# Latent attention with a gated feed-forward network on one core: maxima over adjacent score banks taken in one instruction, and small jobs and rope steps moved between units

## The chip, the cores and the metric

The kernel runs on one core of one Trainium2 chip. The metric is the device time of one execution in microseconds (us), lower being better.

## The reference

The input is x with 2048 tokens of 256 features. After a layer norm it goes through two branches whose product is added to x:

```python
xn = layernorm(x)
# attention, 16 heads, 128 plain + 64 rope features per query and key, latent width 64
q = xn @ wq; kva = xn @ wkv_a
ckv = rmsnorm(kva[:64]) * scale; k_pe = kva[64:]          # one rope key for all heads
k_nope, v = split(ckv @ wkv_b)
scores = causal([q_nope, rope(q_pe)] . [k_nope, rope(k_pe)] * 192**-0.5)
s = (softmax(scores) @ v) @ wo
# feed-forward, 704 hidden features
g = silu(down(silu(xn @ gate) * (xn @ up)))
out = x + s * g
```

## The kernel before, in words

Keys and values stay in latent form for all heads. `K_hi` and `K_lo` hold 64 rope and 64 latent key rows for the 2048 tokens, and each head's queries are brought into the same space (`wabs` is its key weight folded into the query weight, `wvo` its value weight folded into wo). Precision comes from splitting every operand into a high and a low part and multiplying three times.

**Units.** The attention is 8 pairs of heads, a pair is 16 units, so 128 units (`u`, and `k` from 0 to 15 within a pair: the key of all tables below). A unit is one head and one step (0 to 7), and a step takes two tiles of 128 queries: a late one, tile 15 - step, and an early one, tile step. The score columns of a unit are three spans: span 0, keys 0 to 1023 of the late tile; span 1, the remaining 1024 - 128 x step keys of the late tile; span 2, the 128 x (step + 1) keys of the early tile. Together they fill 2176 columns in five PSUM banks (`s_ps`): banks 0 and 1 hold span 0, the next one or two hold span 1, the others hold span 2. There is one copy of them, so unit u + 1 can write a bank only when the exponential of unit u has read it.

**What each engine does, in its own fixed order.** TensorE (PE), loop u: scores of u + 1 for spans 0 and 1, weighted values (`weigh`) of unit u - 2 for span 0, scores of u + 1 for span 2, `weigh` for spans 1 and 2, then the jobs of unit u. VectorE (DVE), loop u: the division by the row sums of a finished unit pair (`normalise`, every second unit), `row_max(u+1, 0)` and `row_max(u+1, 1)`, its part of the jobs of u - 1, the low half of one wide span (`prob_low`), `row_max(u+1, 2)`. ScalarE (ACT), loop u: exponentials of spans 0 and 1 (`exponentials`), high half of span 0 (`prob_high`), exponential of span 2, its part of the jobs of u - 1, in units 3, 5, 11 and 13 also `rope_high` (three copies of rotated query rows, which wait for POOL), high halves of spans 1 and 2. GpSimd (POOL), loop u: low halves of span 0 and of the smaller other span, then the steps that `steps_at(u)` lists. SyncE (SP), loop u: the four copies of `swap` if a `qB` job of u - 1 exists, then the two transposing DMAs of unit u's probabilities (`turn_first`, `turn_rest`), and the loads for the next pair.

**Maxima.** `exponentials` needs the negated row maximum `neg_max`. For the late tile `row_max` takes one maximum of span 0 (L941, as soon as its scores are there), one of span 1 (L941), and combines the two numbers (L944) after a wait on its own result; for the early tile one instruction does it (L939).

**Jobs** are the small matrix products and transposes beside the scores: query projections `qA3` to `qB0` (head A or B, query group 3, 0, 2, 1), weight preparation `wqT`, `wkvT`, `wabs`, `wvo`, outputs `outT` and `outP`. Each writes one of two PSUM slots (`slot_ps`) in turn, and PE waits in `slot` until the job before the last one has been read out by DVE or ACT. The dictionaries `JOBS_BEFORE`, `JOBS_OWN` and `JOBS_NEXT` give the unit of each job of the previous, the same or the next pair, at most two jobs to a unit.

**Rope** of query group g, both heads together: after the job `qBg` ACT has put the unrotated rows into `q_pe`, SP copies them with halves exchanged into `q_swap`, POOL does `rope g.0` (`pe` = q_pe x cos), `rope g.1` (q_swap x sin) and `rope g.2` (their sum), ACT makes the high parts (`rope_high`, fixed units), POOL the low parts (`A2lo`, `B2lo`). `POOL_OWN` and `POOL_NEXT` place the POOL steps:

```python
POOL_NEXT = {1: ["wkvs"], 6: ["wpe_hi"], 7: ["wpe_lo"], 10: rope(3), 11: ["A3lo", "B3lo"], 12: rope(0), 13: ["A0lo", "B0lo"]}
POOL_OWN = {2: rope(2), 3: ["A2lo", "B2lo"], 4: rope(1), 5: ["A1lo", "B1lo"]}
ROPE_HI_OWN, ROPE_HI_NEXT = {3: 2, 5: 1}, {11: 3, 13: 0}
```

Before the attention stand some 80 us of setup, behind it the feed-forward network, from about 985 us on.

Of the kernel before, what the change touches and what calls it, by code (L numbers as in the profile page):

```python
# [99 lines left out]
class Steps:  # L100
# [6 lines left out]
    def after(self, name):  # L107
# [69 lines left out]
def rope(g):  # L177
    return [f"rope{g}.{i}" for i in range(3)]
# [7 lines left out]
POOL_NEXT = {1: ["wkvs"], 6: ["wpe_hi"], 7: ["wpe_lo"], 10: rope(3), 11: ["A3lo", "B3lo"], 12: rope(0), 13: ["A0lo", "B0lo"]}  # L186
POOL_OWN = {2: rope(2), 3: ["A2lo", "B2lo"], 4: rope(1), 5: ["A1lo", "B1lo"]}
# [38 lines left out]
def mla_gated_ffn_kernel(nc, x, wq, wkv_a, wkv_b, wo, kv_scale, gate_w, up_w, down_w, gate_s, up_s,  # L226
                         down_s, cos_in, sin_in, cosT_in, sinT_in, out):
    with ExitStack() as ctx:
# [13 lines left out]
        def ab(name, shape, dt=F32):  # L242
            return sb(name, shape, dt, attn)
# [70 lines left out]
        part_max = ab("part_max", [P, 2, 2])  # L314
# [42 lines left out]
        scores_ready, part_done, max_ready = sem("scores_ready"), sem("part_done"), sem("max_ready")  # L357
# [519 lines left out]
        def _(dve):  # L877
# [392 lines left out]
```

## Time and profile before

| | us |
|---|---|
| median of three runs (lowest, highest) | 1112.69 (1109.94, 1112.72) |
| the profiled execution's own time | 1112.44 |
| its span, first to last instruction | 1110.6 |
| setup / eight pairs / feed-forward, read from the timelines | about 80 / 905 / 126 |
| one pair in the middle (313.08 to 426.64) | 113.56 |

A page's "busy" is the time in which an engine runs an instruction. An entry such as "[3.48 <-POOL pe L1102]" is idle time of the engine just before an instruction and what ended it. L numbers are lines of the kernel before. All element-wise operations of POOL carry L1102 and ACT's copies L725, so they are told apart by the names out<-in. "granted clock" or PEclk is TensorE's clock as a share of its full one.

### The profile page before, as it was taken

What the parts mean: (1) busy time and instruction counts of PE and PEld (TensorE: products, weight loads), DVE (VectorE), ACT (ScalarE), POOL (GpSimd) and SP (SyncE); (2) the same over time, 40 slices, a digit from 0 to 9 for tenths busy, and PEclk for the clock granted to TensorE, in tenths of its full rate; (3) what the DMA queues carried; (4) which work ended last, traced back from release to release, by engine and by line L of the source; (5) the groups of instructions that cost most, each with busy time, mean ns of one, the idle gap of its engine ahead of it and who ended that gap; (6) DMA issues with size and microseconds to landing.
All of it is one profiled execution on the core that took longest, in us unless ns stands there. A gap on an engine that the chain in (4) does not pass through costs nothing.

```text
span 1110.6 us, 26363 instructions
## 1 busy us (share of the span) xinstructions
PE 976.1 (88%) x10560; PEld 842.8 (76%) x10560; DVE 728.5 (66%) x1093; ACT 787.7 (71%) x1157; POOL 711.0 (64%) x514
## 2 busy tenths in 40 slices
PE   5738898989898989898989899998898898779998
PEld 5726786878787878786878787877787777768887
DVE  6546666767776767576767676777676776663134
ACT  1427878788887887787778878878888787763232
POOL 3455958486948694877487857776786667722331
PEclk8759998999999999999999989999899999889999
DMA  5018998989999999999989999999999989992001
GB/s 166 9 48 150 170 178 166 172 163 191 170 177 174 179 173 172 173 178 169 180 165 171 183 166 179 180 173 173 176 167 177 179 159 199 190 180 76 1 19 58
DMA packets 591978, 170.23 MB, mean 153 GB/s; under 512 B 574064, under 2 KB 585968, under 8 KB 591856
## 3 DMA queue, kind: packets, MB, share of 16 engines
q1 hardware_dynamic: 587376, 167.89, 83.7%
q8 instruction: 84, 1.38, 0.5%
q10 hardware_dynamic: 4480, 0.66, 0.4%
q14 instruction: 38, 0.31, 0.1%
HBM read 15.41 MB, written 2.10 MB: 16 GB/s over the span
## 4 chain that ended last, share of the span: by engine, by line
PE 27%; SPq 22%; POOL 16%; ACT 10%; issue 8%; DMA 8%; DVE 7%; ACTq 1%; POOLq 0%
SPq L465 10%; PE s_ps L620 10%; PE s_ps L522 9%; SPq L457 6%; DMA q_swap<-q_pe 5%; POOL hl L1102 5%; ACT hl L725 5%; SPq L451 4%; POOL pe L1102 4%; POOL q_swap L1102 4%; PE slot_ps L522 3%; ACT prob L802 2%; ACT QB_hi L725 2%; DVE part_max L941 2%; DVE hl L950 2%
## 5 line engine op out<-in xcount | busy, mean ns | idle before, releaser
L1102 POOL TENSOR_TENSOR hl<-prob,hl 128x1024 f16<-128x1024 f32 (+4 forms) x256 | 402.1, 1571 | 184.1 <-ACT hl L725 173.1
L802 ACT ACTIVATE prob<-s_ps,neg_max 128x1024 f32<-128x1024 f32 (+7 forms) x384 | 318.0, 862 | 95.1 <-DVE neg_max L944 74.4
L941 DVE TENSOR_REDUCE part_max<-s_ps 128x1 f32<-128x1024 f32 (+7 forms) x256 | 245.5, 988 | 176.6 <-PE s_ps L620 159.4
L725 ACT ACTIVATE hl<-prob 128x1024 f16<-128x1024 f32 (+7 forms) x384 | 296.3, 806 | 9.9 <-DMA pT<-hl 7.9
L636 PE MATMUL o_ps<-v,pT 128*128 128x65 f16 x2176 | 232.0, 195 | 7.1 <-DMA pT<-hl 5.7
L637 PE MATMUL o_ps<-v,pT 128*128 128x64 f16 x2176 | 232.5, 197 | 0.0
L638 PE MATMUL o_ps<-v,pT 128*128 128x65 f16 x2176 | 231.3, 193 | 0.0
L636 PEld LDWEIGHTS o_ps<-v,pT 128*128 128x128 f16 x2176 | 206.5, 98 | 7.8 <-DMA pT<-hl 6.3
L950 DVE TENSOR_TENSOR hl<-prob,hl 128x1024 f16<-128x1024 f32 (+3 forms) x128 | 158.3, 1236 | 78.0 <-ACT hl L725 76.5
L638 PEld LDWEIGHTS o_ps<-v,pT 128*128 128x128 f16 x2176 | 205.7, 100 | 0.0
L637 PEld LDWEIGHTS o_ps<-v,pT 128*128 128x128 f16 x2176 | 205.1, 98 | 0.0
L620 PE MATMUL s_ps<-K_hi,QB_hi 128*128 128x512 f32 (+3 forms) x320 | 133.4, 417 | 73.7 <-ACT prob L802 73.7
L620 PE MATMUL s_ps<-K_hi,QA_hi 128*128 128x512 f32 (+3 forms) x320 | 124.0, 387 | 16.4 <-DVE K_lo L887 9.7
L620 PEld LDWEIGHTS s_ps<-K_hi,QB_hi 128*128 128x128 f32 x320 | 65.9, 206 | 92.1 <-ACT prob L802 82.0
L620 PE MATMUL s_ps<-K_hi,QB_lo 128*128 128x512 f32 (+3 forms) x320 | 125.5, 392 | 0.0
L620 PE MATMUL s_ps<-K_lo,QB_hi 128*128 128x512 f32 (+3 forms) x320 | 124.9, 390 | 0.0
L620 PE MATMUL s_ps<-K_hi,QA_lo 128*128 128x512 f32 (+3 forms) x320 | 117.3, 367 | 0.0
L620 PE MATMUL s_ps<-K_lo,QA_hi 128*128 128x512 f32 (+3 forms) x320 | 117.2, 366 | 0.0
L939 DVE TENSOR_REDUCE neg_max<-s_ps 128x1 f32<-128x256 f32 (+7 forms) x128 | 96.4, 753 | 2.8 <-PE s_ps L623 0.9
L620 PEld LDWEIGHTS s_ps<-K_hi,QA_hi 128*128 128x128 f32 x320 | 61.0, 191 | 28.9 <-DVE K_lo L887 10.1
L725 ACT ACTIVATE QA_hi<-pe 64x512 fp32r<-64x512 f32 x32 | 20.2, 632 | 84.6 <-POOL pe L1102 84.6
L1234 POOL TENSOR_TENSOR hid_lo<-hid,hid_hi 128x512 fp32r<-128x512 f32 x24 | 31.4, 1307 | 74.1 <-ACT hid_hi L725 74.1
(182 smaller groups left out, 1974.8 us busy)
## 6 DMA issues: line engine op xcount, KB each, us to landing
q_swap<-q_pe SPq DMA_DIRECT2D x128, 64.0 KB, 2.1
pT<-hl SPq DMA_TRANSPOSE x256, 4.9
wq_sb<-in_L_attn_wq_dram SPq DMA_DIRECT2D x8, 384.0 KB, 4.1
acc<-in_L_attn_x_dram SPq DMA_DIRECT2D x4, 512.0 KB, 6.3
wo_sb<-in_L_attn_wo_dram SPq DMA_DIRECT2D x8, 256.0 KB, 4.0
x_in<-in_L_attn_x_dram SPq DMA_DIRECT2D x1, 2048.0 KB, 8.3
out_dram<-y SPq DMA_DIRECT2D x8, 256.0 KB, 2.1
wkvs<-in_L_attn_wkv_b_dram SPq DMA_DIRECT2D x8, 128.0 KB, 4.3
```

The lines of the kernel that those rows point to most:

```text
L465: sp.dma_start_transpose(pT12[:, u % 2], hl12[:, u % 2, :]).then_inc(turned12[u % 2], 16)
L522: last = nc.tensor.matmul(out_ap, a, b, start=(i == 0), stop=(i == n - 1))
L620: mm = nc.tensor.matmul(s_ps[:, b, 0:c], a[:, q], kk[:, k0 + c0:k0 + c0 + c], start=(j == 0), stop=(j == 2 and not ends))
L636: nc.tensor.matmul(whole, pT[:, b, :], v[:, kb, 0:LORA + 1], start=(m != 1 and b == 0), stop=False)
L637: nc.tensor.matmul(part, pT[:, b, :], v[:, kb, LORA + 1:VW], start=False, stop=False)
L638: last = nc.tensor.matmul(whole, pT[:, n + b, :], v[:, kb, 0:LORA + 1], start=False, stop=(m > 0 and b == n - 1))
L725: return nc.scalar.activation(dst, src, ACT.Copy)
L802: nc.scalar.activation(prob_of(u, m), score_bank(u, m), ACT.Exp, bias=neg_max[:, r:r + 1]).then_inc(exp_done, 1)
L939: nc.vector.tensor_reduce(neg_max[:, r:r + 1], src, AX.X, ALU.max, negate=True).then_inc(max_ready, 1)
L941: nc.vector.tensor_reduce(part_max[:, u % 2, m:m + 1], src, AX.X, ALU.max).then_inc(part_done, 1)
L950: nc.vector.tensor_tensor(both[:, w:2 * w], prob_of(u, m), both[:, 0:w], ALU.subtract).then_inc(lo_dve, 1)
L1102: return lambda: nc.gpsimd.tensor_tensor(dst, a, b, op)
```

## The change

Three things change. First, `row_max(u, 0)` now waits for the scores of spans 0 and 1, takes one maximum over the columns of both, which are contiguous across banks 0 to 2 or 3, and writes `neg_max` itself; the second maximum, the combination, the tile `part_max` and its semaphore are gone. Second, jobs move between units, most of them one or two units earlier: the query projections, `wkvT`, `wabs`; the output halves of `outP0` and `outP2` are put into two units, `outP1` and `outP3` come one unit earlier. `qA2` now belongs to unit 15 of the pair before, and in the first pair to unit 0 (`JOBS_FIRST`). Third, step 0 of each rope stands one unit earlier on POOL than steps 1 and 2, and for group 3 those stay in unit 10 while its projections come one unit earlier; `wpe_lo` joins `wpe_hi` in unit 6. `rope_high` keeps its units.

```diff
-JOBS_BEFORE = {2: ["outT3"], 4: ["outP3a", "outP3b"]}
-JOBS_OWN = {0: ["qA2"], 1: ["qB2"], 2: ["qA1"], 3: ["qB1"], 5: ["wvo"], 6: ["outT0"], 7: ["outP0a", "outP0b"], 10: ["outT1"],
-            12: ["outP1a", "outP1b"], 14: ["outT2"], 15: ["outP2a", "outP2b"]}
-JOBS_NEXT = {3: ["wqT"], 5: ["wkvT"], 6: ["wabs"], 8: ["qA3"], 9: ["qB3"], 10: ["qA0"], 11: ["qB0"]}
-FFN_COUNT = {8: 1, 9: 2, 10: 1, 11: 2, 13: 2, 14: 1, 15: 2}
+JOBS_BEFORE = {0: ["outP2b"], 2: ["outT3"], 3: ["outP3a", "outP3b"]}
+JOBS_OWN = {0: ["qB2"], 1: ["qA1"], 2: ["qB1"], 5: ["wvo"], 6: ["outT0"], 7: ["outP0a"], 8: ["outP0b"], 10: ["outT1"],
+            11: ["outP1a", "outP1b"], 14: ["outT2"], 15: ["outP2a"]}
+JOBS_NEXT = {4: ["wqT", "wkvT"], 5: ["wabs"], 7: ["qA3"], 8: ["qB3"], 9: ["qA0"], 10: ["qB0"], 15: ["qA2"]}
+JOBS_FIRST = {0: ["qA2"]}
+FFN_COUNT = {8: 1, 9: 2, 10: 1, 12: 2, 13: 2, 14: 1, 15: 2}
...
-POOL_NEXT = {1: ["wkvs"], 6: ["wpe_hi"], 7: ["wpe_lo"], 10: rope(3), 11: ["A3lo", "B3lo"], 12: rope(0), 13: ["A0lo", "B0lo"]}
-POOL_OWN = {2: rope(2), 3: ["A2lo", "B2lo"], 4: rope(1), 5: ["A1lo", "B1lo"]}
+POOL_NEXT = {1: ["wkvs"], 6: ["wpe_hi", "wpe_lo"], 9: rope(3)[:1], 10: rope(3)[1:], 11: ["A3lo", "B3lo"] + rope(0)[:1], 12: rope(0)[1:],
+             13: ["A0lo", "B0lo"]}
+POOL_OWN = {1: rope(2)[:1], 2: rope(2)[1:], 3: ["A2lo", "B2lo"] + rope(1)[:1], 4: rope(1)[1:], 5: ["A1lo", "B1lo"]}
...
             def row_max(u, m):
-                src = score_bank(u, m)
+
                 r = (2 * u + m // 2) % 4
-                dve.wait_ge(scores_ready, scores_through(u, m))
-                if m == 2:
-                    nc.vector.tensor_reduce(neg_max[:, r:r + 1], src, AX.X, ALU.max, negate=True).then_inc(max_ready, 1)
-                    return
-                nc.vector.tensor_reduce(part_max[:, u % 2, m:m + 1], src, AX.X, ALU.max).then_inc(part_done, 1)
-                if m == 1:
-                    dve.wait_ge(part_done, 2 * u + 2)
-                    nc.vector.tensor_reduce(neg_max[:, r:r + 1], part_max[:, u % 2, :], AX.X, ALU.max, negate=True).then_inc(max_ready, 1)
+                src = score_bank(u, 2) if m else s_ps[:, 0:2 + len(banks(u, 1)), :].rearrange("p b c -> p (b c)")[:, 0:W0 + width(u, 1)]
+                dve.wait_ge(scores_ready, scores_through(u, m or 1))
+                nc.vector.tensor_reduce(neg_max[:, r:r + 1], src, AX.X, ALU.max, negate=True).then_inc(max_ready, 1)
...
                 if u + 1 < NU:
                     row_max(u + 1, 0)
-                    row_max(u + 1, 1)
```

The order on the engines moves at three places that matter. The first is DVE at the turn from one pair to the next (L913 reads out an output half `outP`, L897 a query projection; the L950 of before is L945 now). Before:

```order
L941 TENSOR_REDUCE part_max<-s_ps 128x1 x2
L944 TENSOR_REDUCE neg_max<-part_max 128x1
L913 TENSOR_TENSOR acc<-slot_ps,acc 128x2x256 x2
L950 TENSOR_TENSOR hl<-prob,hl 128x1024
L939 TENSOR_REDUCE neg_max<-s_ps 128x1
```

Now, from the same maximum on:

```order
L939 TENSOR_REDUCE neg_max<-s_ps 128x1
L913 TENSOR_TENSOR acc<-slot_ps,acc 128x2x256
L897 TENSOR_TENSOR QA_lo<-slot_ps,QA_hi 64x512
L945 TENSOR_TENSOR hl<-prob,hl 128x1024
L939 TENSOR_REDUCE neg_max<-s_ps 128x1 x2
L913 TENSOR_TENSOR acc<-slot_ps,acc 128x2x256
L897 TENSOR_TENSOR QB_lo<-slot_ps,QB_hi 64x512
```

Two neighbouring units now hold two jobs each, where one held two and the next one. The three maxima of the late tile have become one.

The second is POOL in units 1 and 2 (hl are low halves, pe and q_swap rope steps, POOL's L1102 is L1096 now). Before:

```order
L1102 TENSOR_TENSOR wkvs<-wkvs,scale_sb 64x512
L1102 TENSOR_TENSOR hl<-prob,hl 128x1024
L1102 TENSOR_TENSOR hl<-prob,hl 128x256
L1102 TENSOR_TENSOR pe<-q_pe,cosT 128x512
L1102 TENSOR_TENSOR q_swap<-q_swap,sinT 128x512
L1102 TENSOR_TENSOR pe<-pe,q_swap 128x512
```

Now:

```order
L1096 TENSOR_TENSOR pe<-q_pe,cosT 128x512
L1096 TENSOR_TENSOR wkvs<-wkvs,scale_sb 64x512
L1096 TENSOR_TENSOR hl<-prob,hl 128x1024
L1096 TENSOR_TENSOR hl<-prob,hl 128x256
L1096 TENSOR_TENSOR q_swap<-q_swap,sinT 128x512
L1096 TENSOR_TENSOR pe<-pe,q_swap 128x512
```

The product with the cosines went ahead of unit 1's `wkvs`; two rope steps are left behind unit 2's low halves instead of three.

The third is PE at the end of units 3 and 4 of the first pair (L536 is `wqT`, L540 `wkvT`, the L522 rows here the projection `qB`, which moved to the unit before):

```order
 L637 MATMUL o_ps<-v,pT 128x64
 L638 MATMUL o_ps<-v,pT 128x65
+L536 MATMUL slot_ps<-ident,wq_sb 128x128 x4
+L540 MATMUL slot_ps<-ident,wkvs 128x128 x4
 L620 MATMUL s_ps<-K_hi,QA_hi 128x512
 L620 MATMUL s_ps<-K_lo,QA_hi 128x512
```

Both weight transposes now follow each other in unit 4, where each needs a slot that unit 3's jobs have left.

## Rows read from the trace of the kernel before

**Rows 1.** The page: busy time of each engine over the whole span
```profile
PE 976.1 (88%) x10560; PEld 842.8 (76%) x10560; DVE 728.5 (66%) x1093; ACT 787.7 (71%) x1157; POOL 711.0 (64%) x514
```

**Rows 2.** One pair, 313.08:426.64: engines' busy us, granted clock, DMA share, GB/s
```profile
313.08:426.64 113.56, 103.47 (x1221) 88.77 (x1220) 82.41 (x118) 92.48 (x135) 81.30 (x56) 0.97 0.99 174
```

**Rows 3.** Waits inside that pair: who for whom, us in total, times, longest
```profile
PE s_ps L620 <- ACT prob L802: 9.8, 5, 3.4
...
ACT QA_hi L725 <- POOL pe L1102: 8.6, 4, 3.5
```

**Rows 4.** Timelines of POOL, ACT and DVE around the stall of units 3 and 4
```profile
334.09 1.28 POOL L1102 TENSOR_TENSOR q_swap<-q_swap,sinT 128x512 f32<-128x512 f32 x1 [1.73 <-DMA q_swap<-q_pe]
335.46 1.29 POOL L1102 TENSOR_TENSOR pe<-pe,q_swap 128x512 f32<-128x512 f32 x1
...
336.78 0.63 ACT L725 ACTIVATE QA_hi<-pe 64x512 fp32r<-64x512 f32 x1 [3.48 <-POOL pe L1102]
...
332.41 2.09 DVE L941 TENSOR_REDUCE part_max<-s_ps 128x1 f32<-128x1024 f32 x2 [1.49 <-PE s_ps L620]
...
343.46 1.22 DVE L941 TENSOR_REDUCE part_max<-s_ps 128x1 f32<-128x1024 f32 x1 [1.66 <-PE s_ps L620]
```

**Rows 5.** Windows of 2 us: PE in that stall and just after it
```profile
338.00:340.00 2.00, 0.00 (x0) 0.00 (x0) 0.43 (x1) 1.95 (x5) 0.96 (x2) 1.00 0.89 199
...
342.00:344.00 2.00, 2.00 (x6) 1.60 (x5) 0.54 (x1) 1.96 (x4) 1.84 (x3) 0.50 1.08 177
```

**Rows 6.** Timelines of ACT and DVE around the stall of unit 11
```profile
392.39 0.63 ACT L725 ACTIVATE QA_hi<-pe 64x512 fp32r<-64x512 f32 x1 [1.90 <-POOL pe L1102]
...
389.40 1.56 DVE L941 TENSOR_REDUCE part_max<-s_ps 128x1 f32<-128x1024 f32 x2 [1.41 <-PE s_ps L620]
...
399.62 1.56 DVE L941 TENSOR_REDUCE part_max<-s_ps 128x1 f32<-128x1024 f32 x2 [1.35 <-PE s_ps L620]
```

**Rows 7.** Timeline of DVE, unit 1, up to unit 2's first maximum
```profile
313.08 1.23 DVE L941 TENSOR_REDUCE part_max<-s_ps 128x1 f32<-128x1024 f32 x1 [1.36 <-PE s_ps L620]
314.51 1.22 DVE L941 TENSOR_REDUCE part_max<-s_ps 128x1 f32<-128x1024 f32 x1 [0.21 <-PE s_ps L623]
315.77 0.16 DVE L944 TENSOR_REDUCE neg_max<-part_max 128x1 f32<-128x2 f32 x1
...
319.65 1.23 DVE L941 TENSOR_REDUCE part_max<-s_ps 128x1 f32<-128x1024 f32 x1 [1.19 <-PE s_ps L620]
```

**Rows 8.** DVE instructions by form: the widest and the narrowest maximum
```profile
L941 DVE TENSOR_REDUCE part_max<-s_ps 128x1 f32<-128x1024 f32 x144 | 176.4, 1225 | 171.1 <-PE s_ps L620 159.4 <-PE s_ps L623 11.2
...
L941 DVE TENSOR_REDUCE part_max<-s_ps 128x1 f32<-128x128 f32 x16 | 4.5, 280 | 0.0
```

**Rows 9.** Timelines of DVE and PE where a pair's unit 0 has just ended
```profile
421.41 1.22 DVE L941 TENSOR_REDUCE part_max<-s_ps 128x1 f32<-128x1024 f32 x1 [1.70 <-PE s_ps L623]
...
422.74 0.68 DVE L887 TENSOR_TENSOR oT_lo<-slot_ps,oT_hi 128x512 fp32r<-128x512 f32 x1
...
423.57 0.36 PE L522 MATMUL slot_ps<-wvo_hi,oT_hi 128*128 128x256 f32 x1 [0.19 <-DVE oT_lo L887]
```

**Rows 10.** The chain that ended last, at the turn of a pair
```profile
418.48 1.12 ACT prob L802
...
419.64 1.66 PE s_ps L620 x6
```

**Rows 11.** SP queue lines in one pair: count, ns min/median/max
```profile
L457 SPq DMA_TRANSPOSE pT<-hl x16: 1317/2276/3651, 315.3 to 422.2; - x16
...
L465 SPq DMA_TRANSPOSE pT<-hl x17: 2687/3242/4285, 311.0 to 425.3; - x17
...
L451 SPq DMA_DIRECT2D q_swap<-q_pe x16: 542/583/591, 330.1 to 402.5; - x16
```

**Rows 12.** Timeline of DVE: one low half of 1024 columns, slow and fast
```profile
414.95 2.36 DVE L950 TENSOR_TENSOR hl<-prob,hl 128x1024 f16<-128x1024 f32 x1 [0.23 <-ACT hl L725]
...
423.34 1.22 DVE L950 TENSOR_TENSOR hl<-prob,hl 128x1024 f16<-128x1024 f32 x1
```

More of the change, by code:

```diff
@@ L140, in jobs_at @@
         last = pair == PAIRS - 1
-        if pair > 0:
-            jobs += [(name, pair - 1) for name in JOBS_BEFORE.get(k, ())]
+        jobs += [(name, pair - 1) for name in JOBS_BEFORE.get(k, ())] if pair > 0 else [(name, pair) for name in JOBS_FIRST.get(k, ())]
         jobs += [(name, pair) for name in JOBS_OWN.get(k, ()) if (name, pair) not in OUT_LAST]
@@ L313, in mla_gated_ffn_kernel @@
         identb = ab("identb", [P, P], BF16)
-        part_max = ab("part_max", [P, 2, 2])
         neg_max = ab("neg_max", [P, 4])
@@ L356, in mla_gated_ffn_kernel @@
         swapped, rope_hi = sem("swapped"), sem("rope_hi")
-        scores_ready, part_done, max_ready = sem("scores_ready"), sem("part_done"), sem("max_ready")
+        scores_ready, max_ready = sem("scores_ready"), sem("max_ready")
         exp_done, prob_hi = sem("exp_done"), sem("prob_hi")
```

## The prediction

> **What bounds the kernel now.** I read the page's busy shares first, then one whole pair, then the waits in it, then the timelines where they fall. TensorE (PE) is busy 88% of the span, ACT 71%, DVE 66% [rows 1]. A middle pair takes 113.56 us with PE busy 103.47 at a mean granted clock of 0.97 [rows 2]. A pair is what repeats: seven full turns of it, and a last pair without projections for a next one.
>
> What PE would need at full clock is 103.47 less what the clock cost, 0.03 x 113.56 = 3.4, so 100.1 us. The other 13.5 of a pair are 10.1 of idle time and 3.4 of clock. The waits say where the idle time sits: five waits of PE for an exponential, 9.8 us, and four waits of ACT for POOL's last rope step, 8.6 us [rows 3]. They are one thing. In unit 3 ACT reached `rope_high` and sat 3.48 us until POOL's `pe` was done; SP's copies had been late for POOL by 1.73 before that [rows 4]. ACT works in order, so the exponentials of unit 4 came late, PE stood still (0.00 busy at 338 to 340), and just afterwards its granted clock was 0.50, the lower of its two levels, 1.2 GHz [rows 5]. DVE's first maximum, which starts when span 0 is ready, stands 11.05 us after the one before (332.41 to 343.46) [rows 4]; the calm distance in the same pair is 6.57 (313.08 to 319.65) [rows 7]. Unit 11 repeats it: ACT waits 1.90, and the maxima stand 10.22 apart (389.40 to 399.62) [rows 6].
>
> **Part 1, the rope.** Steps 1 and 2 stay behind the low halves, but step 0, 1.3 us like its neighbours [rows 4], runs a unit earlier, where POOL has idle time, and the copies that feed step 1 are issued a unit earlier. In unit 3 `pe` then ends 1.3 us (the step) plus 1.73 (the wait for the copies) earlier, 3.0 of the 3.48 waited. In unit 11, whose projections too come a unit earlier, the 1.90 goes whole. I take all of the 13.5 us as removed and add back what stays or comes. The bounds of the removal: nothing, if ACT would be late by its own work, and 13.5. I take the upper end because the waits for `pe` in ACT's queue are the rows directly ahead of both large stalls.
>
> What stays for ACT: `rope_high` is three copies of 0.63 [rows 4], 1.9 us. ACT's 92.48 over 16 units [rows 2] less these is 5.3 a unit, 7.2 with them, against PE's 100.1 / 16 = 6.3: 0.9 of backlog in each of four units. After an exponential of span 0 PE has 0.9 to spare (worked out under part 3), which covers three of them. The fourth, unit 13, now follows units 12 and 13 without any job, and jobs are some 1.35 of PE's 6.3, so backlog meets a unit of 4.9: 1.4 us. With 0.3 for unit 5, which gets two weight copies: **1.7 us a pair**.
>
> **Part 2, the maximum by itself.** A maximum of 1024 columns takes 1225 ns, one of 128 takes 280 [rows 8]: 1.055 ns a column and 0.15 us fixed. No row has more than 1024 columns or crosses from span 0 into span 1; extended, 2048 columns take 2.31 us, with 2.31 to 2.45 (two whole ones) as the ends, and I take 2.31 because every form lies on that line. Per unit DVE saves 0.15 fixed and 0.16 for the combination. But it starts later. In unit 1 span 0 was ready at 313.08, span 1 at 314.51, and `neg_max` stood at 315.93, 1.42 after span 1 [rows 7]. Now it stands 2.31 after it: **0.9 later at 2048 columns**, shrinking to about 0.1 at 1152, since then span 1 is ready soon after span 0.
>
> **Part 3, where that is paid.** The first candidate is the exponential. It takes 1.12 for spans of 1024, and six score matmuls of span 0 take 1.66 [rows 10]. So in unit 1 it ends at 315.93 + 1.12 = 317.05, and PE starts the next span 0 at 319.65 - 1.66 = 317.99 [rows 7]: 0.94 of spare against 0.9 more. Just covered; if the cover is gone, each unit pays the difference (the third rival). The second is the slot. A job must wait until DVE has read out the job two before it, which stands behind the maximum in DVE's queue. At the turn of a pair PE got there already 0.19 too early: span 1 ready at 421.41, DVE's job after the maxima at 422.74, PE's matmul at 423.57 [rows 9]. PE alone needs 423.38 - 421.41 = 1.97 from span 1 to its jobs; DVE's path took 2.16, of which 0.94 is not the maximum, 0.79 without the combination. Now it is 2.31 + 0.79 = 3.10, so PE waits 1.13. And the table now puts two jobs into each of units 15, 0, 2, 3, 4 with one in unit 1, so that there is a slot wait in each; before, the units between held one job. Unit by unit (the maximum shrinks by 0.135 a step; PE's way, an estimate, grows by 0.15 because span 2 grows): unit 15, 1.13 - 0.19 = 0.94; unit 0, 1.13; unit 1, 0.85; unit 2, 0.3 (only its second job waits); unit 3, 0.5; unit 4, 0.65, `wqT` and `wkvT` both waiting. From step 3 on the two ways are equal. **Sum 4.4 us a pair.** Ends: 0, if DVE keeps ahead, and 6 x 1.13 = 6.8.
>
> **Part 4, the rest.** A low half on DVE took 1.22 or 2.36 [rows 12], the long one while POOL worked. DVE's later start gives new meetings of that kind; between 0 and 4 a pair, each 1.14; I take about one, **1.0**. The Trainium skill, SBUF — State Buffer, section "Who interferes with whom", says a VectorE instruction with two SBUF inputs contends with a GpSimd one that reads SBUF, that a tensor_reduce never does, and that issue order decides who blocks. By that rule the merged maximum itself stays at its length, and four such meetings in place of one would bring 7 x 3.4 = 24 us on the sum below. SP: medians of 2.28 and 3.24 for the transposes of a unit and 0.58 for a copy [rows 11] make 16 x 5.52 + 16 x 0.58 = 97.6 us a pair; no instruction is added, but the swap moves past one unit's transposes and stands ahead of `turn_first` of units 1, 3, 9, 11. In units 12 and 13, 4.9 long, the queue falls behind by 2 x 0.6, partly buffered by the two copies of the turned tiles: **0.8**. The other moved jobs keep their lengths on every engine and lie inside the 100.1.
>
> **The sum.** A pair: 100.1 + 4.4 + 1.7 + 1.0 + 0.8 = 108.0, against 113.56, so 5.56 less. Seven times that is 39. In the last pair two rope stalls go and the same slot waits come: nothing. 1112.44, the profiled execution's own time, less 39 gives **1073 us**; the median, 1112.69, is the same within 0.3.
>
> **The rivals.** (A) As forecast, 1055 to 1090, chance 0.63.
>
> (B) No slot waits: if span 1's maximum were short enough for PE, a pair takes 103.6 and the time is 1112 - 7 x 10 = 1043. For it speaks that PE waited for a slot only 0.19 before; against, that DVE's queue there leaves no slack at all. The Trainium skill, Perfetto Trace Analysis, section "Identifying the Most-Contended Engine", would have one look at the most occupied engine, and DVE is the third here; by that rule its longer path costs nothing. 0.12.
>
> (C) Slower: ACT's own load, not its wait, makes the stalls. Place: the units after 3, 5, 11 and 13. `exponentials` now starts up to 0.9 later, the spare of 0.94 is used up, so ACT's backlog falls on PE in full and all 13.5 us stay, with the 4.4 of slot waits on top, less the 0.19: 1112 + 7 x 4.2 = 1142. It decides from the point where the rope's move frees less than 4.4 us a pair. ACT is at 81% of the pair, which speaks for it; the wait of 3.48 in one piece speaks against. 0.10.
>
> (D) The change does only half of what it says: SP's queue, with its maxima of 3.65 and 4.29 [rows 11], needs up to 107 us a pair once PE runs on, and it idles for some 4 in units 0 and 1. Then a pair takes 111 and the time is 1095. 0.15.
>
> **How the numbers follow.** Range 1045 to 1103: A and D whole with the second meeting of part 4, and the upper edge of B; left out are C and most of B. A measurement can tell about 0.3%, 3.3 us. Slower is C, 0.10, and 0.02 for mishaps of the new order; 0.04 falls within 0.3%, between D and C; faster 0.84.
>
> **What would show it.** Right: ACT's waits for `pe` under 2 us a pair; no window at a granted clock of 0.50 behind unit 3 or 11; the group of maxima at 2.3 us for 2048 columns; PE waits on `slot_ps` for DVE of 4 us a pair in units 15 to 4; distances of 7 to 8 us between the late tile's maxima there. Wrong: idle PE before `s_ps` still near 10 us a pair (C), `slot_ps` waits near 0 (B), or SP without gaps (D).

## The result: slower by 1.25%, and the profile after

| | before | after |
|---|---|---|
| median, us (lowest, highest) | 1111.44 (1109.94, 1112.72) | 1125.77 (1120.64, 1128.94) |
| ratio to before, 95% interval | | 1.0125 [1.0078, 1.0172] |
| span of the profiled execution, us | 1110.6 | 1127.0 |
| mean granted clock | 0.943 | 0.955 |

The forecast was 1073 us, faster. The changed kernel is slower, outside the range and on the other side. The page of after, busy time and the chain that ended last:

```profile
PE 978.6 (87%) x10560; PEld 840.2 (75%) x10560; DVE 699.3 (62%) x837; ACT 789.3 (70%) x1157; POOL 714.7 (63%) x514
...
PE 36%; DVE 15%; POOL 15%; ACT 13%; issue 8%; DMA 8%; SPq 5%; ACTq 1%; POOLq 0%
```

Against [rows 1] DVE has 256 instructions and 29 us of work less, the others are as they were, and the time is longer. One operation marks the pairs well: the division of a finished unit pair, eight to a pair of heads. The first and the 57th of them, and the last, in DVE's timeline of after:

```profile
116.40 0.17 DVE L954 RECIPROCAL rinv<-o_ps 128x4 f32<-128x4 f32 x1
...
925.20 0.17 DVE L954 RECIPROCAL rinv<-o_ps 128x4 f32<-128x4 f32 x1
...
1016.14 0.18 DVE L954 RECIPROCAL rinv<-o_ps 128x4 f32<-128x4 f32 x1 [7.09 <-PE o_ps L638]
```

and of before:

```profile
112.17 0.17 DVE L959 RECIPROCAL rinv<-o_ps 128x4 f32<-128x4 f32 x1
...
909.54 0.17 DVE L959 RECIPROCAL rinv<-o_ps 128x4 f32<-128x4 f32 x1
...
1000.72 0.18 DVE L959 RECIPROCAL rinv<-o_ps 128x4 f32<-128x4 f32 x1 [8.27 <-PE o_ps L638]
```

The seven turns between the first two take 808.8 us, 115.54 each, against 797.4, 113.91 each. So 11.4 of the 16.4 us of span lie in the turns, 4.2 ahead of them (1.3 of these ahead of the first exponential, 82.92 against 81.64), and 0.7 behind them. This mean of seven turns is called the length of a pair from here on. TensorE over the seven turns, after and before, in the windows view:

```profile
116.40:925.20 808.80, 723.75 (x8545) 618.87 (x8546) 542.88 (x602) 650.24 (x940) 573.58 (x386) 0.99 0.97 172
```

```profile
112.17:909.54 797.37, 725.12 (x8525) 623.47 (x8526) 569.86 (x826) 647.72 (x939) 568.87 (x385) 0.96 0.99 174
```

PE is busy 103.4 us a pair after and 103.6 before; its idle time is 12.15 against 10.32. So the added time is idle time of PE. One middle pair of after in the windows view, for [rows 2]:

```profile
313.46:427.81 114.35, 101.80 (x1220) 87.12 (x1220) 77.89 (x87) 92.84 (x135) 82.41 (x55) 1.00 0.97 174
```

PE is idle for 12.55 us of it, where it was 10.1. The waits in it, for [rows 3]:

```profile
DVE neg_max L939 <- PE s_ps L623: 27.3, 15, 3.4
ACT prob L802 <- DVE neg_max L939: 19.9, 16, 2.5
...
PE s_ps L620 <- ACT prob L802: 8.2, 6, 2.7
ACT QA_hi L725 <- POOL pe L1096: 2.8, 2, 1.6
...
PE slot_ps L522 <- DVE acc L913: 1.8, 2, 1.0
PE slot_ps L522 <- DVE oT_lo L887: 1.6, 2, 1.1
...
PE slot_ps L522 <- DVE QA_lo L897: 0.4, 1, 0.4
...
PE slot_ps L536 <- DVE acc L913: 0.5, 1, 0.5
```

These are the whole account. PE's waits for a slot are 1.8 + 1.6 + 0.5 + 0.4 = 4.3 us, its waits for an exponential 8.2, and 4.3 + 8.2 = 12.5. The slot waits are new and of the size forecast. The waits for an exponential were 9.8 before and should have fallen to about 3.5. DVE's instructions by form, widest and narrowest merged maximum, for [rows 8]:

```profile
L939 DVE TENSOR_REDUCE neg_max<-s_ps 128x1 f32<-128x2048 f32 x16 | 36.7, 2292 | 56.4 <-PE s_ps L623 56.4
...
L939 DVE TENSOR_REDUCE neg_max<-s_ps 128x1 f32<-128x1152 f32 x16 | 21.6, 1350 | 6.2 <-PE s_ps L623 6.2
```

**Where the old stalls went.** ACT's timeline in unit 3 of that pair, for [rows 4]:

```profile
336.67 2.02 ACT L802 ACTIVATE prob<-s_ps,neg_max 128x1024 f32<-128x1024 f32 x2 [1.26 <-DVE neg_max L939]
338.57 1.05 ACT L725 ACTIVATE hl<-prob 128x1024 f16<-128x1024 f32 x1
339.52 0.47 ACT L802 ACTIVATE prob<-s_ps,neg_max 128x256 f32<-128x256 f32 x1
339.87 0.60 ACT L725 ACTIVATE oT_hi<-slot_ps 128x512 fp32r<-128x512 f32 x1
340.50 0.59 ACT L725 ACTIVATE q_pe<-slot_ps 64x512 f32<-64x512 f32 x1
341.11 0.59 ACT L725 ACTIVATE QB_hi<-slot_ps 64x512 fp32r<-64x512 f32 x1
341.72 0.63 ACT L725 ACTIVATE QA_hi<-pe 64x512 fp32r<-64x512 f32 x1
...
343.54 1.26 ACT L725 ACTIVATE hl<-prob 128x896 f16<-128x896 f32 x2
344.82 1.12 ACT L802 ACTIVATE prob<-s_ps,neg_max 128x1024 f32<-128x1024 f32 x1
```

The wait of 3.48 for `pe` is gone, as forecast. But ACT is busy without a gap from one exponential to the next, 344.82 - 336.67 = 8.15 us: this unit carries `rope_high` and three more copies of 0.6 for two jobs. Unit 11 has the same picture, 8.36 us (391.57 to 399.93). It was so before as well: there ACT's exponentials of units 3 and 4 stood at

```profile
328.42 2.02 ACT L802 ACTIVATE prob<-s_ps,neg_max 128x1024 f32<-128x1024 f32 x2 [0.36 <-DVE neg_max L944]
...
339.87 1.91 ACT L802 ACTIVATE prob<-s_ps,neg_max 128x1024 f32<-128x1024 f32 x2
```

and 11.45 less the wait of 3.48 [rows 4] leaves 7.97 us of ACT's own work. In unit 5 the wait is still there. ACT and POOL:

```profile
356.99 0.63 ACT L725 ACTIVATE QA_hi<-pe 64x512 fp32r<-64x512 f32 x1 [1.56 <-POOL pe L1096]
```

```profile
345.69 2.02 POOL L1096 TENSOR_TENSOR QA_lo<-pe,QA_hi 64x512 fp32r<-64x512 f32 x1
347.79 1.28 POOL L1096 TENSOR_TENSOR QB_lo<-pe_b,QB_hi 64x512 fp32r<-64x512 f32 x1
349.15 1.28 POOL L1096 TENSOR_TENSOR pe<-q_pe,cosT 128x512 f32<-128x512 f32 x1
350.51 3.72 POOL L1096 TENSOR_TENSOR hl<-prob,hl 128x1024 f16<-128x1024 f32 x2
354.31 1.28 POOL L1096 TENSOR_TENSOR q_swap<-q_swap,sinT 128x512 f32<-128x512 f32 x1
355.67 1.28 POOL L1096 TENSOR_TENSOR pe<-pe,q_swap 128x512 f32<-128x512 f32 x1
```

POOL has no gap for 11 us here, so step 0 in an earlier unit is still in front of step 2, and the swapped rows, which no longer come late, change nothing. The exponentials stand 9.13 apart (350.83 to 359.96); in unit 13, with the same picture, 9.61 (404.74 to 414.35).

### The profile page after: what moved, and what is told of

The parts are those of the page before. It is cut to its first block, busy times and chain, and to the rows that moved or that the text cites. A ratio compares the mean times of both kernels' runs of the same rounds, so it can differ in the third digit from the quotient of the medians.

```text
span 1127.0 us, 26107 instructions
## 1 busy us (share of the span) xinstructions
PE 978.6 (87%) x10560; PEld 840.2 (75%) x10560; DVE 699.3 (62%) x837; ACT 789.3 (70%) x1157; POOL 714.7 (63%) x514
## 4 chain that ended last, share of the span: by engine, by line
PE 36%; DVE 15%; POOL 15%; ACT 13%; issue 8%; DMA 8%; SPq 5%; ACTq 1%; POOLq 0%
PE s_ps L620 15%; PE s_ps L522 9%; DVE neg_max L939 9%; POOL hl L1096 6%; PE slot_ps L522 6%; ACT hl L725 5%; DMA pT<-hl 5%; ACT prob L802 4%; DVE hl L945 3%; POOL pe L1096 3%; POOL q_swap L1096 2%; ACT QB_hi L725 2%; SPq L465 2%; PE o_ps L522 2%; POOL QA_lo L1096 1%
## 5 line engine op out<-in xcount | busy, mean ns | idle before, releaser
L1096 POOL TENSOR_TENSOR hl<-prob,hl 128x1024 f16<-128x1024 f32 (+4 forms) x256 | 399.5, 1561 | 250.3 <-ACT hl L725 240.5
L939 DVE TENSOR_REDUCE neg_max<-s_ps 128x1 f32<-128x1792 f32 (+15 forms) x256 | 329.0, 1288 | 245.1 <-PE s_ps L623 243.2
L725 ACT ACTIVATE hl<-prob 128x1024 f16<-128x1024 f32 (+7 forms) x384 | 296.5, 807 | 12.7 <-DMA pT<-hl 10.6
L636 PE MATMUL o_ps<-v,pT 128*128 128x65 f16 x2176 | 229.1, 193 | 5.4 <-DMA pT<-hl 3.3
L637 PE MATMUL o_ps<-v,pT 128*128 128x64 f16 x2176 | 229.7, 196 | 0.0
L638 PE MATMUL o_ps<-v,pT 128*128 128x65 f16 x2176 | 228.6, 192 | 0.0
L945 DVE TENSOR_TENSOR hl<-prob,hl 128x1024 f16<-128x1024 f32 (+3 forms) x128 | 161.8, 1264 | 62.0 <-ACT hl L725 59.8
L620 PE MATMUL s_ps<-K_hi,QB_hi 128*128 128x512 f32 (+3 forms) x320 | 129.5, 405 | 46.6 <-ACT prob L802 46.6
L620 PE MATMUL s_ps<-K_hi,QB_lo 128*128 128x512 f32 (+3 forms) x320 | 121.9, 381 | 0.0
L620 PEld LDWEIGHTS s_ps<-K_hi,QB_lo 128*128 128x128 f32 x320 | 64.1, 200 | 10.7
L620 PEld LDWEIGHTS s_ps<-K_lo,QB_hi 128*128 128x128 f32 x320 | 64.1, 200 | 10.5
```

What stands on the lines that cost most here:

```text
L620: mm = nc.tensor.matmul(s_ps[:, b, 0:c], a[:, q], kk[:, k0 + c0:k0 + c0 + c], start=(j == 0), stop=(j == 2 and not ends))
L636: nc.tensor.matmul(whole, pT[:, b, :], v[:, kb, 0:LORA + 1], start=(m != 1 and b == 0), stop=False)
L637: nc.tensor.matmul(part, pT[:, b, :], v[:, kb, LORA + 1:VW], start=False, stop=False)
L638: last = nc.tensor.matmul(whole, pT[:, n + b, :], v[:, kb, 0:LORA + 1], start=False, stop=(m > 0 and b == n - 1))
L725: return nc.scalar.activation(dst, src, ACT.Copy)
L945: nc.vector.tensor_tensor(both[:, w:2 * w], prob_of(u, m), both[:, 0:w], ALU.subtract).then_inc(lo_dve, 1)
```

## The experiments

Ratios are to the kernel before on the same chip in the same minutes. Waits are PE's over the whole run, from the waits view: "exp" for an exponential, "slot" for a slot in the attention. Pair and waits come from one profiled execution each, which can lie some us off the median (6 to 7 below it for e1, g1 and g4, 4 above it for e2). The value of a ratio in us is taken on 1112.

| run | median us | ratio [95%] | pair us | exp | slot |
|---|---|---|---|---|---|
| before | | | 113.91 | 80.4 | 1.4 |
| after | 1125.77 | 1.0125 [1.0078, 1.0172] | 115.54 | 65.9 | 32.1 |
| e1_merge_only | 1121.71 | 1.0100 [1.0069, 1.0130] | 114.61 | 65.7 | 25.6 |
| e2_table_only | 1095.93 | 0.9852 [0.9820, 0.9885] | 112.14 | 67.9 | 3.0 |
| e3_jobs_only | 1109.70 | 0.9985 [0.9971, 1.0000] | 113.94 | 72.8 | 8.5 |
| e4_late_start | 1129.13 | 1.0156 [1.0132, 1.0179] | 116.02 | 59.3 | 37.0 |
| e5_max_first | 1096.33 | 0.9864 [0.9843, 0.9884] | 112.66 | 65.5 | 5.8 |
| e6_two_back | 1097.42 | 0.9877 [0.9859, 0.9894] | 112.17 | 69.4 | 3.0 |
| e7_pool_relief | 1071.72 | 0.9644 [0.9626, 0.9662] | 108.97 | 53.7 | 3.0 |
| e8_after_max_first | 1119.18 | 1.0072 [1.0053, 1.0091] | 115.14 | 55.0 | 32.1 |
| f1_after_relief | 1103.50 | 0.9935 [0.9913, 0.9958] | 112.67 | 49.3 | 32.1 |
| f2_after_jobs_first | 1127.71 | 1.0151 [1.0125, 1.0177] | 115.59 | 94.1 | 0.6 |
| f3_cos_on_dve | 1078.22 | 0.9683 [0.9644, 0.9723] | 109.29 | 54.9 | 3.0 |
| f4_cos_merged_jobs_first | 1117.31 | 1.0059 [1.0037, 1.0081] | 114.33 | 86.2 | 0.6 |
| g1_table_late | 1142.43 | 1.0270 [1.0232, 1.0307] | 117.79 | 63.3 | 43.7 |
| g5_table_merge_narrow | 1093.23 | 0.9817 [0.9790, 0.9845] | 111.65 | 66.1 | 3.0 |
| g6_table_merge_wide | 1124.32 | 1.0113 [1.0073, 1.0154] | 115.83 | 69.8 | 32.1 |
| g4_cos_merge_narrow | 1078.03 | 0.9676 [0.9631, 0.9720] | 109.08 | 55.6 | 3.0 |

### The two halves apart

**e1_merge_only** is the kernel before with the new `row_max` and nothing else.

> The kernel before with the merged maximum alone, its own tables. Theory T1 (the maximum costs: neg_max 0.9 us later at 2048 columns falls on PE through slots and through the exponential): slower, 1118 to 1135 us, the calm distance between late-tile exponentials in units 0 to 3 grows by 0.3 to 0.9 us each, and PE waits on slot_ps for DVE grow from 0.2 to 1 to 3 us a pair. Theory T2 (the maximum is nearly free in the old table, the new table is what costs): within 5 us of before, 1107 to 1116.

**e2_table_only** is the changed kernel with the two maxima and their combination put back: all tables new.

> The kernel after with the two separate maxima and their combination back, all new tables kept. T1: the slot waits of about 4 us a pair go, the rope gain stays, so faster than before: 1080 to 1095 us. T2: the table itself is no better than the old one: 1110 to 1125 us, with the exponentials of units 5 to 6 and 13 to 14 still 9 us apart as they are in the kernel after.

**e3_jobs_only** is e2 with the POOL tables of before:

```diff
+POOL_NEXT = {1: ["wkvs"], 6: ["wpe_hi"], 7: ["wpe_lo"], 10: rope(3), 11: ["A3lo", "B3lo"], 12: rope(0), 13: ["A0lo", "B0lo"]}
+POOL_OWN = {2: rope(2), 3: ["A2lo", "B2lo"], 4: rope(1), 5: ["A1lo", "B1lo"]}
```

> As the table-only kernel, but POOL keeps the order of before: the jobs moved, the rope steps not. T1 (moving rope step 0 ahead is what frees ACT): ACT's wait for POOL's pe in unit 3 comes back with 1 to 3 us and the time is 5 to 20 us above the table-only kernel. T2 (the moved steps stand ahead of the next unit's low half on a POOL that has no room, which costs as much as they bring): equal to the table-only kernel within 5 us, or faster.

The merged maximum costs 11 us on the old tables and 1.0125 - 0.9852, 30 us, on the new ones. The tables bring 16 us. The jobs' moves alone bring 2 (the interval of e3 reaches 1.0000), the POOL moves on top the rest. A part of that rest may only repair what e3 itself opens: its query projections come a unit earlier while `wpe_lo` stays in unit 7, and PE waits 5.5 us over the run for POOL's `wc_lo`, a wait that neither before nor e2 has. The forecast had 70 us for the tables (7 x 13.5, less 3.5 a pair of residues) and -31 for the slots. In e2 a middle pair still has these rows, windows view and waits:

```profile
313.00:425.60 112.60, 103.35 (x1221) 89.24 (x1220) 83.21 (x118) 93.07 (x134) 81.31 (x56) 0.97 1.00 176
```

```profile
PE s_ps L621 <- ACT prob L803: 9.0, 5, 2.7
PE slot_ps L523 <- DVE oT_lo L888: 0.2, 1, 0.2
```

Of the 9.8 us of [rows 3] 9.0 are left, and the clock stays at 0.97. That is the failure of the forecast in one line. PE's timeline says where they sit. Before, the waits behind units 3 and 5:

```profile
341.04 0.50 PE L620 MATMUL s_ps<-K_hi,QB_hi 128*128 128x512 f32 x1 [3.43 <-ACT prob L802]
...
356.08 0.50 PE L620 MATMUL s_ps<-K_hi,QB_hi 128*128 128x512 f32 x1 [0.74 <-ACT prob L802]
```

and in e2, behind units 3 and 5 and in and behind unit 13:

```profile
332.17 0.50 PE L621 MATMUL s_ps<-K_hi,QB_hi 128*128 128x512 f32 x1 [1.11 <-ACT prob L803]
347.11 0.50 PE L621 MATMUL s_ps<-K_hi,QB_hi 128*128 128x512 f32 x1 [2.39 <-ACT prob L803]
...
397.60 0.50 PE L621 MATMUL s_ps<-K_hi,QA_hi 128*128 128x512 f32 x1 [1.52 <-ACT prob L803]
402.90 0.79 PE L621 MATMUL s_ps<-K_hi,QB_hi 128*128 128x512 f32 x1 [2.74 <-ACT prob L803]
```

The two large stalls did shrink, in unit 3 from 3.43 to 1.11 and in unit 11 from 2.45 to 1.21, 3.6 us together. Those of units 5 and 13 grew, from 0.74 to 2.39 and from 1.98 to 1.52 + 2.74 = 4.26, 3.9 us together. (A wait of 1.19 at the end of the pair went.) So the stall moved more than it went.

### What the rest of the stalls is made of

**e6_two_back** is e2 with step 0 of the ropes of groups 1 and 0 back beside the other steps:

```diff
-... 9: rope(3)[:1], 10: rope(3)[1:], 11: ["A3lo", "B3lo"] + rope(0)[:1], 12: rope(0)[1:],
+... 9: rope(3)[:1], 10: rope(3)[1:], 11: ["A3lo", "B3lo"], 12: rope(0),
...
-... 3: ["A2lo", "B2lo"] + rope(1)[:1], 4: rope(1)[1:],
+... 3: ["A2lo", "B2lo"], 4: rope(1),
```

> Table-only kernel with rope step 0 of groups 1 and 0 put back behind the next unit's low halves (units 4 and 12), while those of groups 2 and 3 stay early. T4 (POOL works without a gap from unit 3 to 5 and 11 to 13, so the place of a step within that stretch does not change when its last step ends): within 4 us of the table-only kernel. If moving step 0 ahead did help there, as my forecast took for granted: 5 to 12 us slower.

It makes no difference (0.9877 against 0.9852, intervals overlap, pair 112.17 against 112.14). Where POOL has no gap, a step's place in it is worth nothing.

**e7_pool_relief** is e2 with POOL's sine product cut from 512 columns to one.

```diff
-... tt(q_swap[:, n % 2, :], q_swap[:, n % 2, :], sinT[:, query_cols(g)], ALU.mult)
+... tt(q_swap[:, n % 2, 0:1], q_swap[:, n % 2, 0:1], sinT[:, g * BANK:g * BANK + 1], ALU.mult)
```

> Table-only kernel with rope step 1 cut to one column: the product with the sines is left out for the other 511 columns, POOL is relieved of 1.2 us four times a pair. T4: ACT's waits for pe, 31 us, fall below 10 and the time to 1070 to 1085 us. T3: the waits for pe fall too, but the low halves still meet POOL: 1085 to 1094 us.

Four times 1.3 us less on POOL shorten a pair by 3.2 us and the run by 23. (The other 511 columns are left out, so this kernel computes something else; it only measures what the time on POOL is worth.) Of the 3.2 us 1.3 are idle time of PE; 1.9 are PE's busy time, 101.4 against 103.3 us a pair, with the granted clock over the seven turns at 0.99 against 0.97. Its middle pair:

```profile
297.40:405.82 108.42, 100.86 (x1222) 86.99 (x1221) 83.55 (x118) 93.09 (x136) 77.56 (x55) 1.00 1.03 183
```

The exponentials of unit 5 now stand 8.72 apart (9.79 in e2), those of unit 13 8.67 (9.77), those of unit 3 8.59 (8.74). PE's waits of units 5 and 13 fell from 2.39 to 0.71 and from 4.26 to 3.16. So in units 5 and 13 POOL holds a share of the stall; in unit 3 the distance stays near the 8.15 that ACT's own instructions fill in the timeline above. PE waits 53.7 us for exponentials even here.

**f3_cos_on_dve** relieves POOL as well, with nothing left out: DVE makes the cosine product right behind the low half of `qB`.

```diff
-    return [f"rope{g}.{i}" for i in range(3)]
+    return [f"rope{g}.{i}" for i in (1, 2)]
...
+                    nc.vector.tensor_tensor(pe[:, n % 2, :], q_pe[:, n % 2, :], cosT[:, query_cols(g)], ALU.mult).then_inc(rope_cos, 1)
```

> Table-only kernel in which rope step 0, the product with the cosines, is done by DVE right behind the job qB (0.7 us there, 1.3 on POOL), four times a pair; nothing is left out. If POOL's load makes the remaining stalls, 1072 to 1085 us, close to the pool-relief kernel. If what helps there was only the shorter way from SP's copies to pe: 1090 to 1098 us.

It is 3.2% faster than before and 4.4% faster than the changed kernel. The product, by form, in this kernel and in the one before:

```profile
L909 DVE TENSOR_TENSOR pe<-q_pe,cosT 128x512 f32<-128x512 f32 x32 | 22.7, 709 | 1.0
```

```profile
L1102 POOL TENSOR_TENSOR pe<-q_pe,cosT 128x512 f32<-128x512 f32 x32 | 47.3, 1478 | 9.5 <-issue 7.0
```

**e5_max_first** and **e8_after_max_first** tested another suspect, DVE's early-tile maximum behind its low half, which meets POOL and is then slow (2.29 at 405.82 in after, where POOL was already at work; 1.09 at 414.48, where it began 0.01 ahead of POOL's `QA_lo`, and that took 2.23 in place of 1.28). The two change places in e2 and in the changed kernel:

```diff
-                if 0 <= u < NU:
-                    prob_low(u, 3 - smaller(u))
                 if u + 1 < NU:
                     row_max(u + 1, 2)
+                if 0 <= u < NU:
+                    prob_low(u, 3 - smaller(u))
```

> Table-only kernel (two maxima, new tables) with one swap on DVE: the early tile's maximum of unit u+1 goes ahead of the low half of unit u. Theory T3 (what is left of the stalls comes through DVE: a low half of 2.2 to 2.5 us that meets POOL holds up the early tile's maximum, so ACT's exponential of span 2 and all behind it come late in units 5, 13 and 15): 1075 to 1088 us, ACT's waits for the early tile's neg_max, 37 us, fall below 15, and the exponentials after unit 5 and unit 13 stand under 9 us apart instead of 9.8. Rival T4 (ACT and POOL have no room in these units, whatever DVE does): 1092 to 1100 us.

> The kernel after (merged maximum, new tables) with the same swap on DVE as the first kernel here. If the slot waits set the loss of the merged maximum, it stays 25 to 32 us above the first kernel: 1103 to 1118 us; if the loss ran through the early tile's maximum, the two come within 12 us of each other.

On e2 nothing came of it: ACT's wait for that maximum fell from 36.8 to 7.5 us over the run, its waits for `pe` and for the turning DMAs rose from 31 and 18 to 42 and 32. On the changed kernel it brought 6 us, and the intervals overlap.

### Why the merged maximum costs 30 us

**f1_after_relief** is the changed kernel with e7's edit.

> The kernel after (merged maximum, new tables) with rope step 1 cut to one column as in the pool-relief kernel: the sine product is left out for the other 511 columns. If the two losses are independent (slot waits of about 4.4 us a pair, and POOL's load), the merged maximum costs 25 to 32 us here too: 1097 to 1104 us. If the slot waits only count because POOL is full, or if POOL's stalls hide them: under 1090 us.

0.9935 against e7's 0.9644: the merged maximum costs 32 us with POOL relieved, as it does without. So the two losses are separate and add up.

**f2_after_jobs_first** is the changed kernel, where DVE does its part of the jobs of u - 1 ahead of the merged maximum, so that a slot is free early:

```diff
-                if u + 1 < NU:
-                    row_max(u + 1, 0)
                 if u <= NU:
                     for name in jobs_at(u - 1):
                         job(name)
+                if u + 1 < NU:
+                    row_max(u + 1, 0)
```

> The kernel after, in which DVE reads out the jobs of unit u-1 ahead of the merged maximum of unit u+1, in time in which it only waited for the scores. If PE's waits for a slot are the price of the merged maximum, they fall from about 4 us a pair to under 1 and the time comes to 1095 to 1106 us. If the price runs through the later exponential, it stays at 1118 to 1128 us. A third way: the jobs wait for ACT's copies where ACT is late (units 3, 5, 11), and the maximum now waits behind them: 1105 to 1118.

The slot waits are gone (0.6) and the time is the same. PE now waits 94.1 us for exponentials, 72 times instead of 47. DVE's timeline ahead of unit 1's exponential in the third pair shows the new path:

```profile
318.35 0.69 DVE L897 TENSOR_TENSOR QA_lo<-slot_ps,QA_hi 64x512 fp32r<-64x512 f32 x1 [1.98 <-ACT QA_hi L725]
319.07 2.29 DVE L939 TENSOR_REDUCE neg_max<-s_ps 128x1 f32<-128x2048 f32 x1
```

DVE stands 1.98 for ACT's copy, and the maximum then starts behind it. In this unit the last product of span 1 ended at 318.29 + 0.23 = 318.52, so the maximum starts 0.5 late and `neg_max` stands 2.84 us after span 1, where the changed kernel has 2.29. So f2 frees the slots and makes `neg_max` later at once. It shows that a free slot does not help if the maximum pays for it; no run frees the slots and leaves the maximum where it is.

**f4_cos_merged_jobs_first** joins the three edits: merged maximum, jobs first, cosine product on DVE.

> The kernel after with both repairs: cosine product on DVE, jobs read out ahead of the merged maximum. If both theories hold: within 8 us of the kernel with the cosines on DVE and two maxima, 1072 to 1090 us. If the merged maximum still costs something of its own, 1090 to 1110.

42 us slower than f3, again with the waits at the exponential.

**e4_late_start** and **g1_table_late** test the lateness alone. Both keep the two maxima; the first one also waits for span 1. e4 is on the kernel before, g1 on e2.

```diff
-                dve.wait_ge(scores_ready, scores_through(u, m))
+                dve.wait_ge(scores_ready, scores_through(u, max(m, 1)))
```

> The kernel before, in which the first maximum also waits for span 1: the lateness of the merged maximum without its saving. neg_max comes 1.2 us later than before at 2048 columns, 0.3 later than merged. T1: slower than the merge-only kernel by 2 to 10 us, and most of the merge-only loss is the late start. T2: like the merge-only kernel within 4 us.

> The new tables with two maxima; the only edit is that the maximum of span 0 also waits for the products of span 1, so it starts as late as the merged maximum does, with nothing of DVE's other work or of the slots' jobs changed in order. T5 (the 30 us that the merged maximum costs on the new tables are its lateness: neg_max is ready later, and DVE, whose work between two units cannot run ahead any more, passes that on): 1123 to 1135 us, at least as slow as the changed kernel (1125.8), since the extra instruction is kept. T6 (the price is the single long reduction that holds the slots' jobs back, and lateness alone costs little): 1098 to 1110, near the tables alone (1095.9).

g1 is 46 us slower than e2 by one wait, with the same instructions in the same order. PE pays it in the slots: those waits rise by 40.7 us over the run, the waits for exponentials fall by 4.6. DVE's timeline, unit 1:

```profile
315.57 2.35 DVE L942 TENSOR_REDUCE part_max<-s_ps 128x1 f32<-128x1024 f32 x2 [3.42 <-PE s_ps L624]
317.96 0.15 DVE L945 TENSOR_REDUCE neg_max<-part_max 128x1 f32<-128x2 f32 x1
```

The same place in the changed kernel, with the two job instructions behind it:

```profile
319.32 2.29 DVE L939 TENSOR_REDUCE neg_max<-s_ps 128x1 f32<-128x2048 f32 x1 [3.42 <-PE s_ps L623]
321.53 0.68 DVE L913 TENSOR_TENSOR acc<-slot_ps,acc 128x512 f32<-128x512 f32 x1
322.24 0.69 DVE L897 TENSOR_TENSOR QA_lo<-slot_ps,QA_hi 64x512 fp32r<-64x512 f32 x1
```

`neg_max` stands 1.42 us after span 1 in the kernel before [rows 7], 2.29 in the changed one and 317.96 + 0.15 - 315.57 = 2.54 in g1; in e2 it is 1.41, as before. Pairs of 112.14 (e2), 115.54 and 117.79 us go with these. It is lateness that costs. Joining the instructions gives a part back, by ratio 6 us on the old tables (e4 to e1) and 16 on the new ones (g1 to the changed kernel); it spares an instruction and 0.25 us of the lateness, and the runs do not part the two.

**g5_table_merge_narrow** and **g6_table_merge_wide** put the merged maximum into one half of a pair's units.

```diff
+                merged = step_of(u) >= HALF // 2
+                if merged and m == 0:
+                    return
+                if merged and m == 1:
+                    src = s_ps[:, 0:2 + len(banks(u, 1)), :].rearrange("p b c -> p (b c)")[:, 0:W0 + width(u, 1)]
```

> The new tables, with the merged maximum only in the steps 4 to 7 of a pair (units 8 to 15), where it reads 1536 to 1152 columns; units 0 to 7 keep two maxima. T5a (every unit pays for the lateness, since DVE and ACT alternate in all of them): about half of the 30 us, 1108 to 1113. T5b (the price sits in the first half, where the slots' jobs wait behind a reduction of 1.8 to 2.3 us): 1093 to 1101, no dearer than the tables alone (1095.9), or gained by the instruction left out.

> The mirror image: the merged maximum only in the steps 0 to 3 of a pair (units 0 to 7, 2048 to 1664 columns), two maxima in the rest. T5a: 1108 to 1113 as well. T5b: 1120 to 1127, the whole price. Its difference and that of the mirror image from the tables alone should add up to the 30 us if the halves do not help each other.

(g6 has `<`.) The narrow half costs nothing (0.9817 against 0.9852: 4 us better by the ratios, the intervals overlap), the wide half costs 29 us. The sum, 25, is 5 short of the 30, which the intervals allow.

**g4_cos_merge_narrow** is f3 with g5's edit.

> The fastest version so far (new tables, two maxima, the cosine product on DVE; 1078.2 us) with the merged maximum in steps 4 to 7 only. T5b: 1070 to 1079, since DVE is spared one instruction a unit where nothing waits behind the maximum. T5a: 1088 to 1096.

It equals f3. The best version found is f3, or g4, at 1078 us.

## Why the prediction was wrong, step by step

**What bounds the kernel.** "They are one thing" was half right. PE's stalls did follow ACT's waits for `pe`, but those waits stood in front of two further limits, ACT's own work in units 3 and 11 (7.97 us in unit 3 before, where PE's share of a pair is 6.3) and POOL's gapless stretches ahead of units 5 and 13.

**Part 1, the failed step:** "I take all of the 13.5 us of a pair as removed". The tables alone took 113.91 - 112.14 = 1.8 us off a pair. The shares of the step: the 3.0 of 3.48 in unit 3 did go, and ACT's waits for `pe` fell from 8.6 [rows 3] to 2.8 us, above the 2 that was named as the mark. The time did not follow: the waits behind units 3 and 11 fell by 3.6 us in e2 and those of units 5 and 13 rose by 3.9. The residue for ACT, 1.7 us, was worked out from a mean of 7.2 us for a unit with `rope_high`; the unit that matters took 8.15, because three copies of two jobs fall into it, as they did before. POOL's residue was put at nothing, with no more reason than that step 0 runs "where POOL has idle time"; e7 and f3 show it worth some 3 us a pair. Residues of 1.7 + 1.0 + 0.8 = 3.5 stand against 8.2 us of measured waits for exponentials. Against the forecast pair of 108.0, the measured 115.54 is 7.5 longer: 4.2 of that is idle time of PE (12.15 where 4.4 + 3.5 was forecast), and 3.3 is the other term of the step, the clock. The sum took all 3.4 us of clock as given back and PE at 100.1. PE was busy 103.4 a pair although the granted clock over the seven turns rose from 0.96 to 0.99, and 101.8 in the pair at 1.00.

**Part 2** held: 2.31 forecast for 2048 columns, 2.29 measured, and 1.35 at 1152. `neg_max` came 0.9 later.

**Part 3** held in size: slot waits of 4.4 a pair forecast, 4.3 in the pair and 32.1 over eight of them measured. The cover of 0.94 at the exponential also held in the changed kernel: in units 0 to 4 of the middle pair PE waits for no exponential. But in f2, with the slots freed and the maximum behind the jobs, PE pays the same at the exponential. The merged maximum cost 30 us in all, forecast 31, while on the old tables it costs 11, since PE's waits for exponentials fell there by 14.7 as the slot waits rose by 24; on the new tables they fell by 2.0 against 29.1. That these were stalls which would have come anyway a little later is my reading, not shown.

**Part 4.** A low half took 2.29 (unit 13) and 2.36 (unit 15) where POOL was at work first, and 1.09 and 1.23 otherwise, and the maxima kept their lengths: 2.02 for 1792 columns at 341.58, POOL idle for 3.02 behind its low half, and again 2.02 at 348.77 with POOL at work. By the rule of the Trainium skill, SBUF — State Buffer, section "Who interferes with whom", both should be so, and the trace agrees. It also agrees on the issue order: at 414.48, with DVE first, it was POOL's product that took longer, 2.23. e5 shows that the order of these two instructions on DVE is worth nothing on e2.

**The rivals.** C came nearest: it named ACT's own load, the four units and the slot waits on top, and its condition, that the move frees less than 4.4 us a pair, was met with 1.8. It forecast 1142, since it freed nothing, and it did not have POOL's part. It had a chance of 0.10; ACT's queue in unit 3 of the kernel before, read instruction by instruction, has 7.97 us of ACT's own work and would have given it much more. B is refuted in both halves. The section named there (the Trainium skill, Perfetto Trace Analysis, section "Identifying the Most-Contended Engine") says to optimize the most occupied engine first; that a longer path on DVE then costs nothing was the rival's conclusion, not the section's. Here DVE's busy time fell by 29 us, its share is 62%, and its later result costs 30 us. D did not set the time: in the changed kernel ACT waits 10.6 us and PE 3.3 us for the turning DMAs over the run, and SP's `turn_first` itself waits 122.1 us for POOL's low halves. But ACT's waits for the turning DMAs, 18.4 us over the run in e2, are 33.3 in e7 and 35.2 in f3, so SP's queue is a candidate for the next limit.

**The marks.** Right: no window below a granted clock of 0.99 in the middle pair of the changed kernel, maxima at 2.3, slot waits at 4, distances of 7 to 8 in units 0 to 2 (8.19, 7.88, 7.14 between exponentials). Not met: ACT's waits for `pe` under 2 us, which were 2.8. The mark for C, "idle PE before `s_ps` still near 10 us a pair", is nearest to what came: 8.2.

**Open.** Which of the POOL moves brings e2's other 15 us (e6 excludes step 0 of groups 1 and 0; `wpe_lo`, for which e3 waits 5.5 us, and groups 2 and 3 are left), whether the merged maximum would be free if the slots were freed without making it later, and what the 54 us of waits for exponentials in f3 are made of beside unit 3.

## What to carry to other kernels

A wait directly ahead of a stall is an upper bound for what its removal brings, not the size. Before counting it as gone, add up the waiting engine's own instructions between the two events in that very unit, with everything the change moves into it, and the releaser's queue likewise; a mean over units, or a busy share of 64%, hides a stretch without a gap. When two instructions on an engine become one, ask when the result that others need is ready: here the early start of the first was worth 46 us, and joining the two gave 16 of them back.

## What the runs showed that I had not expected

PE's granted clock. The slower kernel had the higher mean, 0.955 against 0.943: its middle pair has 12.55 us of idle PE at a clock of 1.00, the pair of before 10.1 at 0.97 [rows 2]. The length of one wait does not tell them apart: before, the clock fell to 0.50 behind waits of 3.43 and 2.45 us, in e2 behind 2.39 and 2.74, and in the changed kernel a wait of 2.75 (up to 415.50) was followed by no fall. What decided it is not shown. Nor did the higher clock shorten PE's busy time over the seven turns, 103.4 us a pair against 103.6. And a product of 128x512 in fp32 took 1.48 us on average on GpSimd before (1.29 in the changed kernel) and 0.71 on VectorE, so that an engine at 66% could take it from one at 64% with profit.
